# A routed expert kernel: ScalarE multiplies the numbers of two of the last four tiles, the counts lie between the slots' steps, the first block begins on high parts, and the third gather is issued ahead of the second scale

## What is computed

```
x = x + xattn(layernorm(x), ctx, ctx, mask, gamma, beta)      # softmax(q k^T / 16) v, then a norm
h = layernorm(x)
gate = softmax(h @ w_gate)                # 8 experts; the best 2 are kept and made to sum to 1
gu = einsum('bsd,edh->ebsh', h, w_gate_up);  g, u = split(gu)
y = einsum('ebsf,efd->ebsd', silu(g) * u, w_down)             # F = 1024
x = x + einsum('bse,ebsd->bsd', gate, y)
```

## Time and profile before

| | |
|---|---|
| time before, median of 3 runs | 436.49 us (436.16 to 436.55) |
| the profiled execution's own time | 436.5 us |
| its span | 434.8 us |
| TensorE (PE) busy | 424.1 us, 98% |
| VectorE (DVE) busy | 304.3 us, 70% |
| ScalarE (ACT) busy | 216.3 us, 50% |
| GpSimd (POOL) busy | 195.7 us, 45% |

### The profile page before, as it was taken

How to read it: one execution, slowest core, us unless ns; L and a number is a source line. 1 busy time by engine, 2 the same in 40 slices (tenths; PEclk the granted TensorE clock), 3 DMA queues, 4 the chain that set the end, 5 groups by cost and what they waited for, 6 DMA issues and landing times.

```text
span 434.8 us, 10143 instructions
## 1 busy us (share of the span) xinstructions
PE 424.1 (98%) x2356; PEld 351.8 (81%) x2356; DVE 304.3 (70%) x749; ACT 216.3 (50%) x461; POOL 195.7 (45%) x217
## 2 busy tenths in 40 slices
PE   9999889999999999999999999999999999999995
PEld 5798457888888888888888888888888888888885
DVE  3878988885886478868856568858785567865633
ACT  3796636554563366365443356536634346434431
POOL 5463253554563434544543455544554444444312
PEclk9999999999999999999999999999999999999999
DMA  7785514452454125425531115442542225112212
GB/s 208 215 258 149 212 42 153 129 167 75 121 135 134 26 73 145 148 31 129 158 98 26 25 26 134 142 114 73 153 140 34 36 65 136 26 25 28 37 13 26
DMA packets 28621, 44.17 MB, mean 102 GB/s; under 512 B 2833, under 2 KB 22219, under 8 KB 28587
## 3 DMA queue, kind: packets, MB, share of 16 engines
q1 hardware_dynamic: 20358, 32.96, 23.8%
q0 software_dynamic: 7520, 10.41, 14.1%
q10 hardware_dynamic: 709, 0.32, 0.3%
HBM read 34.04 MB, written 9.65 MB: 100 GB/s over the span
## 4 chain that ended last, share of the span: by engine, by line
PE 92%; DVE 3%; ACT 2%; DMA 1%; issue 1%; POOL 0%; DVEq 0%; POOLq 0%
PE bank L1440 48%; PE bank L1463 16%; PE bank L1465 8%; PE bank L1453 8%; PE bank L1238 3%; PE bank L1424 2%; PE bank L1284 1%; PE bank L1307 1%; PE bank L1317 1%; PE bank L1270 1%; DMA tok<-rows_d,gather_i 1%; PE bank L1510 1%; ACT ctxT L1109 1%; DVE x_sb L702 1%; PE bank L1529 0%
## 5 line engine op out<-in xcount | busy, mean ns | idle before, releaser
L1440 PE MATMUL bank<-w,tokT_hi 128*128 (+1 forms) x616 | 170.0, 398 | 1.2 <-DVE tokT_lo L920 0.9
L1160 ACT ACTIVATE gated<-bank,row_rstd 128x512 f32<-128x512 f32 x77 | 53.0, 688 | 173.8 <-PE bank L1440 173.8
L1440 PEld LDWEIGHTS bank<-w,tokT_hi 128*128 128x128 f32 x616 | 110.0, 188 | 22.9 <-DVE tokT_lo L920 1.2
L1463 PE MATMUL bank<-w,aT_hi 128*128 (+1 forms) x304 | 116.4, 417 | 0.1
L929 DVE SCALAR_TENSOR_TENSOR act<-bank,row_rstd,gated 128x512 f32<-128x512 f32 x77 | 57.6, 749 | 78.3 <-ACT gated L1160 78.3
L588 POOL DMA_INDIRECT out<-y_sb,out_i x39 | 62.1, 1592 | 89.0 <-DVE y_sb L950 85.6
L1440 PE MATMUL bank<-w,tokT_lo 128*128 (+1 forms) x308 | 95.3, 390 | 0.0
L1465 PE MATMUL bank<-w,aT_lo 128*128 (+1 forms) x304 | 85.3, 281 | 0.0
L575 POOL TENSOR_TENSOR tok<-tok,beta_b 128x256 f32<-128x256 f32 x36 | 26.3, 730 | 97.3 <-DMA tok<-rows_d,gather_i 97.3
L1440 PEld LDWEIGHTS bank<-w,tokT_lo 128*128 128x128 f32 x308 | 57.8, 188 | 12.9
L1463 PEld LDWEIGHTS bank<-w,aT_hi 128*128 128x128 f32 x304 | 57.2, 188 | 10.4 <-DVE w L402 0.4
(11 more groups left out here) (190 smaller groups left out, 413.8 us busy)
## 6 DMA issues: line engine op xcount, KB each, us to landing
raw<-in_L_ffn_w_gate_up SPq DMA_DIRECT2D x32, 512.0 KB, 3.7
raw<-in_L_ffn_w_down SPq DMA_DIRECT2D x16, 512.0 KB, 3.7
rows_d<-x_sb SPq DMA_DIRECT2D x8, 265.0 KB, 4.7
x_sb<-in_x SPq DMA_DIRECT2D x8, 256.0 KB, 7.6
out<-x_sb SPq DMA_DIRECT2D x8, 256.0 KB, 4.7
out<-y_sb,out_i POOLq DMA_INDIRECT x39
tok<-rows_d,gather_i POOLq DMA_INDIRECT x38, 3.7
cap<-in_mask_BxSxS_ik SPq DMA_DIRECT2D x1, 462.0 KB, 6.3
```

Source lines behind the costliest of these rows:

```text
L1160: act_e.activation(gated[:, h, :], ps_g[h][:, :], ACT.Silu, scale=row_rstd[:, s:s + 1]).then_inc(gated_set, 1)
L1440: ins = pe.matmul(ps[:, :], tokens_[:, s, k, :], w.rearrange("p a g d -> p (a g) d"), start=(k == 0 and tokens_ is tokT_hi and part == 0), ...
L1463: pe.matmul(ps_y[:, :], aT_hi[:, h, c, :], w.rearrange("p a t d -> p (a t d)"), start=(h == 0 and c == 0), stop=False, skip_group_check=True)
```

## The change

Four edits, with what each does.

1. The last group of four tiles is halved. ACT multiplies the numbers into the far two tiles (`FAR`), DVE into the near two only. DVE's comparison with the high digit is made for the near half and then for the far half, and TensorE's products of the far tiles wait for a fourth `token_set` and for ACT's `place_set`.
2. Four steps that turn the counts into padded counts are moved between the steps of `slots` of the last group. `ends` and `jump` move ahead of `gather_0`.
3. ACT splits the fifth weight piece and loads the Silu table before the numbers of the second group instead of behind them.
4. The first product of a block waits for `tokT_hi`; in the first block the low part is waited for where it is read. POOL issues the third gather ahead of the second block's scale.

```diff
+    FAR = GROUPS[-1][len(GROUPS[-1]) // 2:]
...
             row_scale(0)
             split_table()
+            gather(2, gather_i[:, 2:3])
             row_scale(1)
-            gather(2, gather_i[:, 2:3])
             gather(3, gather_i[:, 3:4])
...
                 dve.tensor_tensor(slot_c[:, part, :], ps_rank[:, part, :], chosen[:, part, :], ALU.mult).then_inc(rank_read, 1)
+                if last:
+                    step(tables, dve.tensor_scalar(count_up[:], ps_count, float(P - 1), None, ALU.add))
...
             def select(i, g):
 
-                if i == len(GROUPS) - 1:
-                    dve.wait_ge(lo_set, i + 1)
-                    dve.tensor_tensor(halved(place_of_group[i]), halved(place_of_group[i]), over_slots(number_4, g), ALU.mult).then_inc(last_place, 1)
                 match(token_of_group[i], g, neg_hi).then_inc(token_set, 1)
+
+            def select_last(i, g):
+
+                near, far = g[:len(g) // 2], g[len(g) // 2:]
+                dve.wait_ge(lo_set, i + 1)
+                part = halved(place_of_group[i][:, 0:columns(near), :])
+                dve.tensor_tensor(part, part, over_slots(number_4, near), ALU.mult).then_inc(last_place, 1)
+                match(token_of_group[i][:, 0:columns(near), :], near, neg_hi).then_inc(token_set, 1)
+                match(token_of_group[i][:, columns(near):columns(g), :], far, neg_hi).then_inc(token_set, 1)
...
             numbers(0, GROUPS[0])
-            numbers(1, GROUPS[1])
             split_high(act_e, 4)
             act_e.activation(silu_ready[:], neg_half[:, 0:1], ACT.Silu)
+            numbers(1, GROUPS[1])
+            numbers(2, FAR)
             split_high(act_e, 5)
...
                 for t in g:
+                    if t == FAR[0]:
+                        pe.wait_ge(token_set, i + 2)
+                    if t in FAR:
+                        pe.wait_ge(place_set, GROUPS[-1][0] + t - FAR[0] + 1)
...
                 if h == 0:
+                    pe.wait_ge(tokT_hi_set, b + 1)
+                if h == 0 and later(b, 1):
                     pe.wait_ge(tokT_lo_set, b + 1)
...
                     for tokens_, part in ((tokT_hi, 0), (tokT_hi, 1), (tokT_lo, 0)):
+                        if not later(b, 1) and h == 0 and tokens_ is tokT_lo:
+                            pe.wait_ge(tokT_lo_set, b + 1)
```

More of the change, by code:

```diff
@@ L736, in slots @@
                 dve.wait_ge(rank_ps, i + 1)
+                last = i == len(GROUPS) - 1
                 dve.tensor_tensor(slot_c[:, part, :], ps_rank[:, part, :], chosen[:, part, :], ALU.mult).then_inc(rank_read, 1)
+                if last:
+                    step(tables, dve.tensor_scalar(count_up[:], ps_count, float(P - 1), None, ALU.add))
                 dve.wait_ge(rank_read, i + 1)
@@ L740, in slots @@
                 step(route, dve.tensor_reduce(both[:, part], slot_c[:, part, :], X, ALU.add))
+                if last:
+                    after(tables)
+                    step(tables, dve.tensor_scalar(blocks_i[:], count_up[:], P.bit_length() - 1, None, ALU.arith_shift_right))
                 after(route)
                 step(route, dve.tensor_tensor(slot[:, part, 0], both[:, part], slot[:, part, 1], ALU.subtract))
+                if last:
+                    after(tables)
+                    step(tables, dve.tensor_scalar(padded[:], blocks_i[:], float(P), float(P), ALU.mult, ALU.max))
                 after(route)
                 step(route, dve.tensor_scalar(hi[:, part, :], slot[:, part, :], 0.5 - P / 2, ROUND, ALU.add, ALU.add))
+                if last:
+                    after(tables)
+                    step(tables, dve.tensor_tensor(cum_part[:], up_to[:], padded[:].unsqueeze(1).to_broadcast([P, E, E]), ALU.mult))
                 after(route)
@@ L823, in block_columns @@
                 after(tables)
-                step(tables, dve.tensor_scalar(jump[:], padded[:], -1.0 / P, float(FULL), ALU.mult, ALU.add))
                 step(tables, dve.tensor_tensor(past[:], block_start[:].unsqueeze(2).to_broadcast([P, NBLK, E - 1]), per_block(ends, P), ALU.is_ge))
@@ L888, in _ @@
             places(2, GROUPS[2])
-            select(2, GROUPS[2])
-            step(tables, dve.tensor_scalar(count_up[:], ps_count, float(P - 1), None, ALU.add))
+            select_last(2, GROUPS[2])
             after(tables)
-            step(tables, dve.tensor_scalar(blocks_i[:], count_up[:], P.bit_length() - 1, None, ALU.arith_shift_right))
-            after(tables)
-            step(tables, dve.tensor_scalar(padded[:], blocks_i[:], float(P), float(P), ALU.mult, ALU.max))
-            after(tables)
-            step(tables, dve.tensor_tensor(cum_part[:], up_to[:], padded[:].unsqueeze(1).to_broadcast([P, E, E]), ALU.mult))
+            step(tables, dve.tensor_reduce(ends[:], cum_part[:], X, ALU.add))
+            step(tables, dve.tensor_scalar(jump[:], padded[:], -1.0 / P, float(FULL), ALU.mult, ALU.add))
             dve.wait_ge(token_ps, len(GROUPS))
@@ L901, in _ @@
             dve.tensor_tensor(gather_0[:], ps_token[:, 0:1], spare_0[:], ALU.add).then_inc(gather_0_set, 1)
-            after(tables)
-            step(tables, dve.tensor_reduce(ends[:], cum_part[:], X, ALU.add))
-            after(tables)
             block_columns()
```

## The result

The changed kernel takes 434.71 us (median of 20 runs, 433.84 to 438.41), the kernel before 436.16 us in its 20 runs. The ratio is 0.9971, 95% interval 0.9960 to 0.9982: 1.3 us faster, 0.8 to 1.7. The forecast was 1.1 us, its range 434.8 to 436.2; against the 436.49 us that the forecast started from, 0.9971 is 435.2, inside it. The profiled execution took 434.75 us, its span is 433.0.

The account below looks back on a forecast made before the run. Only the lead-up to the first expert products and three TensorE waits (1.4 us together) could give time. Terms 0.46 + 0 + 0.45 + 0.2 = 1.1 us took 436.5 to 435.4 us; range 434.8 to 436.2.

Parts of the forecast that it names:

- First term: Lead-up to the first expert products: `gather_0` 0.35 earlier, centring at 58.50 behind the gather's landing, a gain of 0.46 us.
- the counts alone bring nothing before `gather_0`: DVE before the first gather: the counts had covered its wait for token products, so removing them alone gains nothing there.
- ScalarE's order: Piece and table load before the second group's numbers: they fill 2.38 us of idle time, overrun by 0.08, cost nothing.
- The rival with a tail behind the table load: ScalarE stays occupied behind the table load, delaying the far tiles' numbers; 436.3 us with a 1.28 tail; chance 0.06.
- the last piece's split end 0.9 earlier: On ScalarE, the last weight piece's split ends 0.9 us sooner, so `table` no longer stands behind it.
- High parts first: First block: the first product's gain is lost at the seventh, with a new wait of 0.4 to 0.5; worth 0.
- Third gather: Third transposes at 72 us: issuing it 3.2 us sooner removes TensorE's wait, 0.45, and the `issue` wait behind, 0.2.
- aren't near TensorE's next need: SP's weight loads follow DVE's low parts, shift with the lead-up's gain, and were taken not to hold TensorE up.
- a sign of being wrong: The forecast is wrong if TensorE waits again between the third transposes and the end; two other signs were named.
- Sum: Whole kernel: 0.46 + 0 + 0.45 + 0.2 = 1.1 us, from 436.5 to 435.4 us.
- The slower rival: First block: TensorE falls to 1.2 GHz after its two idle stretches, giving 438.5 us; chance 0.05.
- The clock never fell: Argument against TensorE slowing in the first block: full clock held through 0.93 and 0.56 us of idling.

Follow-up runs that it names:

- e11: The changed kernel with the last group whole again, all four tiles multiplied and compared at once on DVE: 434.53 us, one run.
- e5: The changed kernel with the four count steps back behind the comparisons and `ends` and `jump` behind `gather_0`: 434.81 us, one run.
- e6: The changed kernel with ScalarE's weight piece and table load back behind all the numbers: 436.56 us, one run.
- e4: The changed kernel with the first block waiting for the low parts of the tokens, as before: 434.63 us, ratio 0.9967.
- e8: The changed kernel with the fourth weight piece's low part made ahead of block 0's two small gate steps: 436.06 us, one run.
- e7: The changed kernel with block 1's first activations and the low part of block 0's second half ahead of the two weight pieces: 433.75 us, ratio 0.9950.
- e2: The kernel before with only the third gather issued ahead of the second scale: 435.55 us, ratio 0.9987.
- e9: e7's edits on the changed kernel; in block 0 the fourth piece's low part and second centring first, then register loads, then gate steps: 433.81 us, ratio 0.9943.
- e10: The changed kernel with the fourth piece's low part, then the two register loads, ahead of block 0's gate steps: 435.05 us, one run.

## Why the prediction was right, point by point

**First term, 0.46.** Measured: 0.46 at the seventh product, by the steps that were named. Behind `slot_c`, `gather_0` moved by 0.40 (forecast 0.35), the gather lands 2.75 us after its issue (2.7), the centring by 0.45, now behind a wait of 0.28 for it (0.2 to 0.3). The counts cost 0.01 where 0.04 was taken. VectorE's wait for the gather took the place of VectorE's own work, and so the block table's 0.82 (`column_sel` from 6.12 to 5.30) brought only this. The forecast had said that the counts alone bring nothing before `gather_0`, and e11 agrees; that the halves without the counts bring only 0.21 at the seventh product it hadn't, and e5 showed it.

**ScalarE's order, 0.** The second group starts 0.75 ahead of `slot_c` in both (50.32 and 51.07; 50.66 and 51.41): there was no overrun, where 0.08 had been taken. The rival with a tail behind the table load is refuted: the load at 48.91 lasts 1.28 and `silu_ready` follows 0.01 behind its end, as the load itself starts 0.02 behind the piece ahead of it (47.85 + 1.04).

The Trainium skill's drain (ScalarE: Activation LUTs, "What ACT_TABLE_LOAD costs") doesn't show here either; the trace decides.

The edit has a worth that the forecast saw only in part: without it (e6) the seventh product comes 1.3 us later than in the change and 0.8 later than in before. The forecast let the last piece's split end 0.9 earlier; by its own terms (56.57, and 53.37 + 0.83 + 1.04 = 55.24) it is 1.3, and behind `slot_c` it measured 1.34.

**High parts first, 0.** Measured 0: 0.9 us earlier at the first product, of which 0.46 is the first term, then a wait of 0.37 before the seventh, whose releaser is the fourth piece's low part (`w`, L403). e4 shows that it brings nothing, e8 why.

**Third gather, 0.45 and 0.2.** The mechanism was right and both sizes were too small. The wait at the third transposes was worth 0.51 (21.47 to 20.50, less 0.46), and the `issue` wait 0.39 (from the first product behind the transposes to the half 1.86 before, 1.47 now) instead of 0.2. The listed idle time, 0.34 and 0.23, is counted from the modelled end of a product, but in a stream the next one starts some 0.16 before it (in before, a product of 0.28 starts at 71.19 and the next at 71.31). The forecast had allowed 0.1 for this at the first wait and nothing at the second. Then 0.42 of the 1.42 gained by then was given back before the third block: this is the step that failed, the sentence that the weight loads "aren't near TensorE's next need". The forecast itself had named it a sign of being wrong that TensorE waits again between the third transposes and the end, and it did. The chain of the change, 67 to 75 us:

```profile
67.40 3.75 DMA raw<-in_L_ffn_w_gate_up
...
71.42 1.07 ACT w L396
...
74.13 0.63 DVE act L940
...
74.81 0.66 PE bank L1473 x4
```

A weight piece for a later expert lands at 71.15, ScalarE makes its high part until 72.49, VectorE its low part until 74.1, and only then comes block 1's activation (74.00 to 74.74), for which TensorE's transposes wait until 74.81, and the low part (ending 75.35) for which the down products wait until 75.40. In before TensorE reached this place 1.27 us later (76.42 - 51.41 = 25.01, now 23.74), and the same chain was hidden: the activation was done at 76.06.

```profile
75.31 0.75 DVE L929 SCALAR_TENSOR_TENSOR act<-bank,row_rstd,gated 128x512 f32<-128x512 f32 x1
76.42 0.60 PE L1453 MATMUL bank<-ident,act 128*128 128x128 f32 x4
```

The view of waits doesn't list the two new waits, as little of them lies behind the modelled end of a product. The starts show them (the transposes 0.73 behind the products ahead of them, the down products 0.59 behind the transposes, in e7 0.45 and 0.36), and e7 takes both away by order alone.

**Sum.** 0.46 + 0.51 + 0.39 + 0.06 between the transposes and their follower, which makes 1.42 at the half, less the 0.42 given back, is 1.0 us by the traces, 1.3 (0.8 to 1.7) by the times, forecast 1.1. The errors were 0.3 too little on the gather's side and 0.4 forgotten behind it. They nearly cancelled, and that is luck: the first term was right for its reasons, the total only because two errors met.

**The slower rival** didn't come in the profiled execution: the granted clock is full in all slices, and the two waits in the first block, 0.47 and 0.37, are together shorter than the one of 0.93. The granted clock alone doesn't settle it, for the profile shows it as 1.00 also over the first eight filler products, which take 0.45 us each, and seven later ones take 0.24. The products do: four of the first block take 1.20 us (59.62), as 1.19 in before. "The clock never fell" holds for the trace that the forecast read, not for every execution: in e2's profile it fell in attention, after 1.12 us of idling, which cost about 3 us. From 56 to 80 us it is 1.00 in all thirteen profiles, also in e8, where TensorE idles for 1.38 us there. So the length of the idling alone doesn't decide it, and what does stays open.

**Open:** whether the 0.3 us between the times and the traces is more than noise (the interval holds both), and what makes two of thirteen profiles 0.5 us slower in the same products.

## What to carry to other kernels

An edit that starts an engine earlier is worth what the next wait on its path leaves of it; so list for each product all of its releasers with the time at which each comes true, and not only the one that comes last now. When two pieces of work run side by side and each hides the other, shortening one of them brings little; both have to be shortened. After a wait is removed, look one or two steps further for a chain that had been hidden by exactly that much, above all for work with no hurry (here weights of a later expert) that stands ahead of work that is waited for, and swap them.

## What the runs showed of the hardware

- Two register loads on VectorE (L965) take 1.8 us from the start of the first to the end of the last in the change (60.3 to 62.1), in e8 (61.5 to 63.3) and in e9 (60.5 to 62.3), and 1.4 us in e10 (60.0 to 61.4). Steps already issued run meanwhile; in the change the 1.21 us step of 60.37 does. What stands behind the loads starts after their end (62.14, 63.35, 62.41, 61.49). So they show as 0.55 us of idle time in the change, 1.67 in e8, 1.17 in e9 and almost none in e10. In the change, e8 and e10 the first load starts within 0.1 us of the start of the last step ahead that had to wait (60.24, 61.46, 59.95). That this sets their start is a reading that fits; it wasn't tested by itself.
- Idle time of TensorE in the list of waits understates what its removal brings by about 0.16 us per wait (0.34 and 0.23 listed, 0.51 and 0.39 gained), as a product in a stream starts before the modelled end of the one ahead.
- TensorE's granted clock fell to 0.50 (1.2 GHz) from 18 to 24 us in e2's profile, after 1.12 us of idling, and the execution took 438.5 us where the median of that kernel is 435.55. In e8, 1.38 us of idling (until 64.33) left it at 1.00.
- Two executions of one program differed by 0.5 us in where attention ended and by 0.49 us (0.14%) in the pace of 338 us of unbroken products. Eleven of thirteen profiles have one pace within 0.05 us, two are 0.5 us slower.
